# A deformable gather on Trainium2: VectorE sums corner by corner over all nine taps, and a fourth corner buffer lies over the tokens

## What is computed

```python
def _L0_conv_ref(x, pw_w, off_w, off_b, dw_w):
    xp = jnp.einsum('bchw,oc->bohw', x, pw_w)
    off = jnp.einsum('bchw,oc->bohw', xp, off_w) + off_b[None, :, None, None]
    off = off.reshape(B, K * K, 2, H, W)
    ...
    sampled = _bilinear_gather(xp, y, xc)      # out += g * weight, for each of 4 corners
    return jnp.einsum('bckhw,ck->bchw', sampled, dw_w.reshape(C, K * K))

x = x + _L0_conv_ref(_gn(x), ...)   # then L1 (7x7 involution), L2 (deformable 3x3), L3 (attention)
```

## Time and profile before

| | us |
|---|---|
| median of 3 timed runs | 2173.13 |
| lowest, highest | 2167.44, 2173.97 |
| span of the profiled execution | 2306.6 |

### The profile page before, as it was taken

One profiled execution on the slowest core, in us unless ns is written; L12 is line 12 of the kernel. 1 busy time (PEld: TensorE's weight loads), 2 busy tenths in 40 slices (PEclk: granted clock), 3 DMA queues, 4 the chain that ended last, 5 costly groups with the idle time before them and its releaser, 6 DMA issues.

```text
span 2306.6 us, 35479 instructions
## 1 busy us (share of the span) xinstructions
PE 1729.9 (75%) x11841; PEld 913.7 (40%) x11841; DVE 1749.1 (76%) x4137; ACT 1186.2 (51%) x3185; POOL 1097.1 (48%) x1232
## 2 busy tenths in 40 slices
PE   4011112116998988786689999999999999999998
PEld 2011111113554456564434444444444444444443
DVE  5477778777999786784587767777788888888881
ACT  3222222210000145556447877787777777777777
POOL 4676777652666355566386766676513000000000
PEclk8555555556999978998779999999999999999999
DMA  8565566540000144446243332333202101020101
GB/s 266 180 186 176 178 184 188 171 135 5 1 1 1 47 135 145 125 151 217 75 124 92 107 90 88 103 104 96 59 10 35 22 19 30 15 34 14 27 1 42
DMA packets 90855, 212.15 MB, mean 92 GB/s; under 512 B 18512, under 2 KB 43824, under 8 KB 90544
## 3 DMA queue, kind: packets, MB, share of 16 engines
q0 software_dynamic: 51840, 169.91, 24.1%
q1 hardware_dynamic: 38832, 39.97, 7.7%
HBM read 175.21 MB, written 13.37 MB: 82 GB/s over the span
## 4 chain that ended last, share of the span: by engine, by line
PE 43%; ACT 3%; DVE 2%; issue 2%; POOL 1%; another core or an unknown queue 0%; SPq 0%; DMA 0%; ACTq 0%; POOLq 0%
PE ps L1801 13%; PE ps L1839 13%; PE ps L1817 11%; ACT l_e L1547 2%; PE ps L1897 2%; DVE l_mx L1671 1%; PE ps L1824 1%; PE ps L1887 1%; ACT corner L1518 1%; PE ps L1851 1%; PE ps L1857 0%; POOL l_part L1414 0%; POOL corner L1405 0%; PE ps L1878 0%
## 5 line engine op out<-in xcount | busy, mean ns | idle before, releaser
L1671 DVE TENSOR_REDUCE l_mx<-ps 128x1 f32<-128x384 f32 x1728 | 837.5, 550 | 162.7 <-PE ps L1817 145.2
L1547 ACT ACTIVATE l_e<-ps 128x384 f32<-128x384 f32 x1728 | 727.0, 511 | 250.0 <-PE ps L1801 236.4
L1817 PE MATMUL ps<-l_ka,l_qs 96*128 96x384 bf16 x1728 | 574.4, 334 | 16.7 <-DMA l_qs<-l_part 8.7
L1801 PE MATMUL ps<-l_qs,l_ks 99*128 99x384 bf16 x1728 | 565.9, 332 | 23.9 <-ACT l_e L1547 18.3
L810 DVE SCALAR_TENSOR_TENSOR m_prod<-ps,c_b,pad 128x384 f32<-128x384 f32 x588 | 325.3, 611 | 77.1 <-PE ps L1015 59.4
L529 PE MATMUL ps<-c_ident,l_samp 128*128 128x128 f32 x324 | 78.5, 427 | 406.2 <-DVE l_samp L392 314.3
L1839 PE MATMUL ps<-l_e,l_v_s 128*32 128x384 f32 x3456 | 336.1, 495 | 2.0 <-ACT l_e L1547 1.0
L1801 PEld LDWEIGHTS ps<-l_qs,l_ks 99*128 99x128 bf16 x1728 | 165.7, 97 | 397.1 <-ACT l_e L1547 216.1
L1444 POOL CAST l_nsp<-l_nm 128x3 bf16<-128x3 f32 x96 | 18.3, 191 | 545.0 <-DVE l_nm L1676 495.2
L250 POOL DMA_INDIRECT corner<-table,idx x216 | 223.1, 1033 | 105.2 <-issue 62.3
L1015 PE MATMUL ps<-red,c_w 32*128 32x384 f32 x1176 | 200.6, 584 | 50.0 <-DVE m_prod L810 40.4
(11 more groups left out here) (212 smaller groups left out, 1961.0 us busy)
## 6 DMA issues: line engine op xcount, KB each, us to landing
corner<-table,idx POOLq DMA_INDIRECT x540
l_ka<-l_part SPq DMA_DIRECT2D x96, 72.0 KB
l_ks<-l_part SPq DMA_DIRECT2D x96, 72.0 KB
table<-l_tok SPq DMA_DIRECT2D x8, 640.0 KB, 6.4
table<-red SPq DMA_DIRECT2D x8, 640.0 KB, 4.9
l_qs<-l_part SPq DMA_DIRECT2D x90, 48.0 KB
l_qs<-l_part SPq DMA_DIRECT2D x96, 24.0 KB
out<-x_map SPq DMA_DIRECT2D x12, 192.0 KB, 1.9
```

What stands on the lines that cost most here:

```text
L1547: nc.scalar.activation(e[:, w % 2, i, :], ps[:, st_bank(at), 0:QC], ACT.Exp).then_inc(s["st_free"], 1)
L1671: nc.vector.tensor_reduce(mx[:, ga % MAX_SLOTS, u // NQC, u % NQC:u % NQC + 1], ps[:, ab_bank(at), 0:CH], AX.X, ALU.max) \
L1801: nc.tensor.matmul(ps[:, bank, 0:QC], ks[:, head % 2, kt * 128:(kt + 1) * 128], qs[:, gb % 3, j * QC:(j + 1) * QC], start=True, stop=True) \
L1817: nc.tensor.matmul(ps[:, bank, 0:CH], qs[0:KROWS, ga // CT % 3, q0:q0 + 128], ka[:, head % 2, k0:k0 + CH], start=True, stop=True).then_inc ...
```

## The change

Three things, all in the first layer:

- VectorE's order. `sum_corners(i, j)` now does one corner j over all nine taps of tile i. The loop calls it for j = 1, then does the by-channel product of the tile before, `by_channel(i - 1)`, then j = 2 and j = 3. The wait on `partial` is now for the same group's sums of the corner before, with at least two groups of other sums in between. `summed` of a group is raised by its corner 3, so for all three groups in the last third of the tile.
- Four corner buffers (`SLOTS` = 4). The fourth lies over the first 4608 numbers per partition of `tok`, the tokens. GpSimd therefore waits, before tile 3, until the second image's table has been written from `tok`.
- The sample ring stays at three (`SAMPS` = 3); ScalarE, VectorE and TensorE now index it by `i % SAMPS`.

The core of the diff:

```diff
-SLOTS = 3
+SLOTS = 4
+SAMPS = 3
...
+        fourth = tok[:, :, :, :].rearrange("p b t c -> p (b t c)")[:, 0:K2 * 4 * 128].rearrange("p (k c) -> p k c", k=K2)
+        corners = [g["corner2"][:, 0, :, :], g["corner2"][:, 1, :, :], third, fourth]
...
+                    if i == SLOTS - 1:
+                        pool.wait_ge(filled[1], 16 * len(COPIES) * PARTS)
...
-                    if i >= SLOTS:
-                        act.wait_ge(s["out_mm"], i - SLOTS + 1)
+                    if i >= SAMPS:
+                        act.wait_ge(s["out_mm"], i - SAMPS + 1)
...
-                def sum_corners(i):
+                def sum_corners(i, j):
                     slot = i % SLOTS
                     for gr in range(GROUPS):
-                        dve.wait_ge(s["first_corner"], i * GROUPS + gr + 1)
-                        for j in range(1, 4):
-                            if j > 1:
-                                dve.wait_ge(s["partial"], 2 * (i * GROUPS + gr) + j - 1)
-                            for k in range(gr * GK, (gr + 1) * GK):
...
+                        if j == 1:
+                            dve.wait_ge(s["first_corner"], i * GROUPS + gr + 1)
+                        else:
+                            dve.wait_ge(s["partial"], (2 * i + j - 2) * GROUPS + gr + 1)
+                        for k in range(gr * GK, (gr + 1) * GK):
...
                     if i < ALL_TILES:
-                        sum_corners(i)
-                        if i == 0:
-                            dve.wait_ge(g["rest_loaded"], 16 * (len(CONSTS) - FIRST))
-                        by_channel(i)
+                        sum_corners(i, 1)
+                    if i == 1:
+                        dve.wait_ge(g["rest_loaded"], 16 * (len(CONSTS) - FIRST))
+                    if 0 < i <= ALL_TILES:
+                        by_channel(i - 1)
+                    if i < ALL_TILES:
+                        sum_corners(i, 2)
+                        sum_corners(i, 3)
```

More of the change, by code:

```diff
@@ L199 @@
 SAMPLE_SEMS = GN_SEMS + ("zeroed pw_mm image off_mm offs tok_mm tok ot_mm chain index table0 table1 "
-                         "gap gaps gather00 gather01 gather02 gather10 gather11 gather12 gather20 gather21 gather22 "
+                         "gap gaps gather00 gather01 gather02 gather10 gather11 gather12 gather20 gather21 gather22 gather30 gather31 gather32 "
                          "first_corner partial summed weighed out_mm added passed border moments level padded "
@@ L223, in sampling_layer @@
         qi = sb("qi", [128, TILES * K2])
-        samp = sb("samp", [128, SLOTS, K2, 128])
+        samp = sb("samp", [128, SAMPS, K2, 128])
         zero = sb("zero", [GUARD, TWIDE])
@@ L227, in sampling_layer @@
         third = sb("corner", [128, K2, 4 * 128])
-        corners = [g["corner2"][:, 0, :, :], g["corner2"][:, 1, :, :], third]
+        fourth = tok[:, :, :, :].rearrange("p b t c -> p (b t c)")[:, 0:K2 * 4 * 128].rearrange("p (k c) -> p k c", k=K2)
+        corners = [g["corner2"][:, 0, :, :], g["corner2"][:, 1, :, :], third, fourth]
         xg = g["red"][:, 0:N]
@@ L320, in first_corner @@
                             w = (i * K2 + k) * 4
-                            ins = nc.scalar.activation(samp[:, slot, k, :], corners[slot][:, k, 0:128],
+                            ins = nc.scalar.activation(samp[:, i % SAMPS, k, :], corners[slot][:, k, 0:128],
                                                        ACT.Copy, scale=wts[:, w:w + 1])
@@ L372, in _ @@
                     dve.wait_ge(s["index"], 2 * b + 2)
-                def sum_corners(i):
+                def sum_corners(i, j):
                     slot = i % SLOTS
                     for gr in range(GROUPS):
-                        dve.wait_ge(s["first_corner"], i * GROUPS + gr + 1)
-                        for j in range(1, 4):
-                            if j > 1:
-                                dve.wait_ge(s["partial"], 2 * (i * GROUPS + gr) + j - 1)
-                            for k in range(gr * GK, (gr + 1) * GK):
-                                w = (i * K2 + k) * 4 + j
-                                last = nc.vector.scalar_tensor_tensor(
-                                    samp[:, slot, k, :], corners[slot][:, k, j * 128:(j + 1) * 128],
-                                    wts[:, w:w + 1], samp[:, slot, k, :], ALU.mult, ALU.add)
-                            last.then_inc(s["partial" if j < 3 else "summed"], 1)
+                        if j == 1:
[3 more added lines that the diff above has]
+                        for k in range(gr * GK, (gr + 1) * GK):
+                            w = (i * K2 + k) * 4 + j
+                            at = samp[:, i % SAMPS, k, :]
+                            last = nc.vector.scalar_tensor_tensor(
+                                at, corners[slot][:, k, j * 128:(j + 1) * 128],
+                                wts[:, w:w + 1], at, ALU.mult, ALU.add)
+                        last.then_inc(s["partial" if j < 3 else "summed"], 1)
                 def by_channel(i):
                     dve.wait_ge(s["summed"], (i + 1) * GROUPS)
-                    at = samp[:, i % SLOTS, :, :]
+                    at = samp[:, i % SAMPS, :, :]
                     nc.vector.tensor_tensor(at, at, g["dw"][:, :, :], ALU.mult).then_inc(s["weighed"], 1)
@@ L528, in _ @@
                     for k in range(K2):
-                        last = nc.tensor.matmul(ps[:, 4 + i % OUTS, 0:128], samp[:, i % SLOTS, k, :], g["ident"][:, :],
+                        last = nc.tensor.matmul(ps[:, 4 + i % OUTS, 0:128], samp[:, i % SAMPS, k, :], g["ident"][:, :],
                                                 start=(k == 0), stop=(k == K2 - 1), is_transpose=True)
```

## The result

| us | before | changed |
|---|---|---|
| median of the timed runs | 2173.55 (4 runs) | 2274.53 (4 runs) |
| lowest, highest | 2167.44, 2177.13 | 2266.89, 2277.95 |
| span of the profiled execution | 2306.6 | 2276.1 |

The changed kernel is slower: its time is 1.047 of that of before (95% interval 1.0441 to 1.0499), some 101 us more. The forecast was 2178 with a range up to 2190.

The account below looks back on a forecast made before the run. The prediction took the timed gather stage as paced by GpSimd, with VectorE waiting for gathers. Reordering 0, buffer 0 and tail +5 us on 2173.1 gave 2178 us, range 2138 to 2190.

Parts of the forecast that it names:

- the late signals: News of finished instructions reaching VectorE and TensorE late; taken as profiling only. Rival that timed runs have them: 2133 us, chance 0.17.
- The 58.7 us: Gather stage without late signals: GpSimd's 37.2 us of waits gone, and 29.2 us after the last issue becoming 7.7.
- the tail: End of the gather stage: last product 7.7 us after the last gather's issue before; the new order adds 4.8, taken as 5.
- The reordering at 0 us: VectorE's sums corner by corner: saves 0.75 us per tile, 27 us over 36 tiles, but hidden behind GpSimd, so 0.
- the fourth buffer: GpSimd may run four tiles ahead in the gathers: worth 0 if never stopped, up to 37.2 us as traced.
- the later release: All three groups' corner buffers come free in the tile's last third; GpSimd wants them three tiles (36 us) later: cost 0.
- the table wait: Tile 3's gathers wait for the second table, as the fourth buffer lies over the tokens: 19 us of cover, cost 0.
- the sums themselves are held: Rival: in slow stretches one VectorE sum gets through per gather issue; fourth buffer lengthens the first stretch: 2186 us, chance 0.14.
- TensorE's late signal: TensorE's matmuls end at 399.8 us, ScalarE resumes at 410.61 with VectorE; used against the SBUF port page's 2186, for 2178.
- No time in front of corners 2 and 3: Sign in the changed kernel's profile: VectorE has no idle time before the sums of corners 2 and 3 in quiet tiles.
- GpSimd's waits gone: Sign in the changed kernel's profile: GpSimd's waits for VectorE's sums fall well below 37 us.
- The 27 sums in 7.3 us: Sign in the changed kernel's profile: VectorE's 27 sums of a quiet tile take about 7.3 us, where they took 7.91.

Follow-up runs that it names:

- second profile of before: The kernel before, unchanged, profiled a second time: time 2170.38 us, span 2168.6 us, against 2306.6 in the first profile.
- the kernel with all waits back: The changed kernel with a wait before every three sums for the three just before, and one on each side of the product: 2162.88 us, 0.9956 of before.

## Why the prediction was wrong, and where it was right

**What bounds the kernel: right.** GpSimd paces the timed stage, and the late signals are not in the timed runs. The second profile of before shows it directly. The 58.7 us that the stage should lose without them was 45.7. Of its parts, the tail was right: the last product now ends 7.7 us behind the last gather, as predicted. The last gather came only 24.2 us earlier, not 37.2. A GpSimd that never pauses meets the product more often (0.84 us per tile instead of 0.56 in the first profile), which gives 10 of these 13 us back.

**The reordering at 0 us: this is the step that failed.** Its own price was right for VectorE: 18 sums take 4.81 us unbroken, 0.262 from start to start (predicted 0.266), and a wait costs 0.13 more (predicted 0.107). But I asked only what it does for VectorE, and found that VectorE has time to spare. That GpSimd's 12.0 us per tile would stay was taken over without a word. They became 15.05, 2.74 more than in the second profile, times 36 about 99 us. By the end of the last gather's issue it is 96.7 us (572.0 against 475.3), and with the tail's 4.6 the 101 us of the timed runs are complete. The other terms held: the fourth buffer 0 (0.9997), the later release 0 (no wait of GpSimd), the table wait 0, the tail +4.6 (12.3 against 7.7) where I had 4.8. So one term of about 99 us stood at zero, and the rest was right.

**The rival "the sums themselves are held": right about the place, wrong about who.** It took the meeting of VectorE and a gather issue and made VectorE the one that waits. Here the gather waits. The row that says so stood in the prediction: the issue of 1.61 us in the earlier trace rows. It begins at 123.68 and ends at 125.29. The product of the earlier trace rows runs from 123.11 and ends at 124.47, 0.82 us before. Had I laid these two ends side by side, as with the 0.81 above, half of the mechanism would have been there: an issue that meets such an instruction can end 0.8 us after it. That a hold can go on from one instruction to the next is not in that row, so the other half was to be asked, not read: what if it does? The longest such stretch after the change is 4.8 us of unbroken sums. An issue that begins 1.25 us into them and is held to their end takes 4.8 + 0.8 - 1.25 = 4.35 us instead of 0.95. That is 3.4 us per tile and 122 us over 36 tiles if every tile has one, where 99 were measured, and it belonged in the prediction as the price of a rival.

The Trainium skill has part of this. "SBUF — State Buffer", section "Who interferes with whom", says that a VectorE instruction with two SBUF inputs contends with a GpSimd instruction that reads SBUF, and that the issue order decides who is blocked. The same section infers that generating a DMA's descriptors needs only the write side, so that a `tensor_tensor` doesn't stall it. The runs differ from that: the product is a `tensor_tensor`, and the issue beside it takes 1.92 us instead of 0.95. I set against it that TensorE's late signal is nothing of that port. That was true, and was no argument: the late signals and the port were two things, and doing away with the first says nothing of the second. The runs bear the page out on the inputs (with one of two from PSUM the sums hold nothing). On the length they go beyond it: for VectorE's two-port modes the page gives the port to whoever comes first for a whole instruction, and here an issue sat out some 14 of them ((102.0 - 98.4) / 0.262). "VectorE: DVE Perf Modes", section "The DRAIN you can't avoid", found eight tensor copies equally long with and without a semaphore after each, so that it costs nothing extra. For these sums it costs VectorE 0.13 us, and the kernel with all waits back loses 3.1 us less per tile behind sums than the changed one.

**What I said would show it.** No time in front of corners 2 and 3, GpSimd's waits gone, and the last product behind an add: all three came true, and the kernel was 101 us slower. They were signs of VectorE's side alone. None of them looked at the duration of a gather issue. The 27 sums in 7.3 us can't be read, since VectorE waits within corner 1 in every tile.

## What to carry to other kernels

Where GpSimd issues gathers and sets the pace, look at how long VectorE runs without a pause on instructions with two SBUF inputs. A gather that is caught by such a run pays for the rest of it, so runs should be short, and long ones cut by a wait or into smaller pieces, even if VectorE gets slower by it. Whether a gather is caught can hang on a few hundredths of a microsecond, so a long run that costs nothing today may cost its full length after an edit elsewhere. A wait that seems to be a pure cost to an engine that isn't the bound may be the gap through which the bounding engine gets its turn, so before it is removed, ask what the other engines do in it. And take the end of each unusually long instruction of the bounding engine and look for what ended just before it: a constant distance is a mechanism, and an edit that lengthens the one side lengthens the other.

## What the runs showed of the hardware that I had not expected

- A gather issue of GpSimd (128 rows of 2 KB) takes 0.95 us when nobody interferes, and 4.42 us when 4.81 us of unbroken VectorE sums catch it. It ends 0.81 us after they do.
- An issue is held behind a single instruction of two SBUF inputs too (1.36 us of product: 1.92 us), and not at all by sums that read one input from PSUM.
- Whether an issue is caught goes by where in a single sum it begins: 127 of 168 at 0.14 to 0.17 us and 33 of 52 in the first 0.03 us were held to the end of the row, and none of 377 elsewhere. At 0.14 to 0.17 us it was none of nine in the first four sums of a row and all 57 from the eighth on.
- One profiled execution of the same kernel was 138 us longer than another (2306.6 against 2168.6), with late signals on VectorE and TensorE. Its idle times led to a right guess here, but a second profile settles such a thing in one run.
